# Hyperbolic attention in a four-stage layer: e to the minus x as VectorE's reciprocal of e to the x, in place of ScalarE's second exponential

## The reference

```python
def poincare_fully_connected(x, z, r, c):          # c = 1
    lam = 2.0 / (1.0 - c * sum(x * x))
    z_norm = maximum(norm(z, axis=0), EPS)
    inner = x @ (z / z_norm)
    v = 2.0 * z_norm * arcsinh(lam * inner * cosh(2 r) - (lam - 1.0) * sinh(2 r))
    w = sinh(v)
    return w / (1.0 + sqrt(1.0 + c * sum(w * w)))
Q, K = poincare_fully_connected(x, z_q, b_q, C), poincare_fully_connected(x, z_k, b_k, C)
V = x @ w_v.T + b_v
scores = einsum('bhqd,bhkd->bhqk', Qh, Kh) / sqrt(D_K)        # 16 heads of 16
out = einsum('bhqk,bhkd->bhqd', softmax(scores), Vh)
```

## Time and profile before

| what | value |
|---|---|
| median of 3 runs | 3054.15 us (3049.62 to 3060.38) |
| profiled execution, its own time | 3049.65 us |
| its span, first to last instruction | 3047.8 us |
| ScalarE busy over the span | 2020.5 us (66%) |
| TensorE busy | 2722.6 us (89%) |
| VectorE busy | 1872.9 us (61%) |
| GpSimd busy | 1281.3 us (42%) |
| attention loop, first to last probability | 1446.3 to about 2650 us |

### The profile page before, as it was taken

The page is one execution under the profiler, slowest core; times in us unless marked ns, Lnnn a source line. Parts: engine busy times, 40 slices in busy tenths (PEclk is TensorE's granted clock), DMA queues, the critical chain, the costliest instruction groups (busy, mean ns, idle before and its releaser), DMA issues. The chain is left out here.

```text
span 3047.8 us, 53922 instructions
## 1 busy us (share of the span) xinstructions
PE 2722.6 (89%) x20897; PEld 1231.4 (40%) x20897; DVE 1872.9 (61%) x2420; ACT 2020.5 (66%) x2650; POOL 1281.3 (42%) x786
## 2 busy tenths in 40 slices
PE   2799989999997999953999999999999999789997
PEld 1355555555554444321333333333333332244443
DVE  8899999999994445356455554555555441144444
ACT  6454554555433655531989999999999999745564
POOL 3798998899892122025323232323232220022110
PEclk7899999999998999976999999999999999989999
DMA  2010010001003121123455554545454546232112
GB/s 83 1 35 25 24 41 28 28 28 34 14 21 105 42 69 55 55 82 66 74 96 101 90 106 83 113 78 119 77 119 74 109 70 123 55 96 70 42 41 69
DMA packets 164051, 201.20 MB, mean 66 GB/s; under 512 B 16504, under 2 KB 118272, under 8 KB 163840
## 3 DMA queue, kind: packets, MB, share of 16 engines
q1 hardware_dynamic: 163840, 198.25, 28.8%
HBM read 139.49 MB, written 58.72 MB: 65 GB/s over the span
## 5 line engine op out<-in xcount | busy, mean ns | idle before, releaser
L1870 ACT ACTIVATE b_pr<-b_ps 128x1024 f32<-128x1024 f32 x1024 | 1000.2, 1035 | 141.9 <-PE b_ps L1889 136.1
L1889 PE MATMUL b_ps<-b_st 128*32 128x512 bf16 x8192 | 610.0, 381 | 36.1 <-ACT b_pr L1870 27.8
L1955 PE MATMUL b_acc<-b_pr,b_vaug 128*32 128x512 f32 x4096 | 529.4, 592 | 3.5 <-DVE b_osb L1758 3.2
L1889 PEld LDWEIGHTS b_ps<-b_st 128*32 128x32 bf16 x8192 | 178.9, 95 | 592.0 <-ACT b_pr L1870 357.1
L1257 PE MATMUL f_po<-f_s,f_w 128*128 128x512 f32 x768 | 353.4, 602 | 9.6 <-DVE f_xr L1042 5.9
L1030 DVE TENSOR_TENSOR f_turned<-f_cs,f_s 128x1024 f32<-128x1024 f32 x96 | 119.4, 1243 | 364.0 <-ACT f_cs L1159 359.0
L635 PE MATMUL a_pv<-a_xnT,a_wv 128*128 128x512 f32 x512 | 252.0, 616 | 53.1 <-DVE a_mem L403 38.9
L1123 ACT ACTIVATE f_h<-f_po,f_b 128x512 f32<-128x512 f32 x192 | 131.9, 687 | 216.5 <-PE f_po L1257 216.5
L627 PE MATMUL a_pu<-a_xnT,a_wk 128*128 128x512 f32 x512 | 236.7, 606 | 29.4 <-DVE a_frac L355 23.4
L1586 POOL TENSOR_TENSOR b_SQ<-b_A 128x1024 f32<-128x1024 f32 x32 | 66.7, 2084 | 454.8 <-DVE b_A L1683 454.8
L674 PE MATMUL a_py<-a_wo,a_out 128*128 128x256 f32 x960 | 229.0, 382 | 0.0
(11 more groups left out here) (261 smaller groups left out, 4548.3 us busy)
## 6 DMA issues: line engine op xcount, KB each, us to landing
b_st<-b_scratch SPq DMA_DIRECT2D x512, 128.0 KB, 7.1
b_scratch<-b_parts SPq DMA_DIRECT2D x32, 768.0 KB, 5.2
f_xl<-x SPq DMA_DIRECT2D x16, 1024.0 KB, 5.5
f_xr<-x SPq DMA_DIRECT2D x16, 1024.0 KB, 6.8
a_xl<-in_L_attn_a_x_dram SPq DMA_DIRECT2D x16, 512.0 KB, 4.2
x<-a_xr SPq DMA_DIRECT2D x32, 256.0 KB, 2.2
x<-f_xr SPq DMA_DIRECT2D x8, 1024.0 KB, 4.5
b_xl<-x SPq DMA_DIRECT2D x8, 1024.0 KB, 9.2
```

Source lines behind the costliest of these rows:

```text
L1870: nc.scalar.activation(pr[:, 4 * (blk % 2) + j, :], ps[:, j % 2, :], ACT.Exp, scale=SC).then_inc(S["probs_done"], 1)
L1889: x = nc.tensor.matmul(o[r:r + 32], w[:, r:r + 32], v, start=start, stop=stop, skip_group_check=True)
L1955: x = nc.tensor.matmul(acc[32 * j:32 * j + 32, h * 512:(h + 1) * 512], vaug[:, kt, c:c + 32], pr[:, 4 * (kt % 2) + j, h * 512:(h + 1) * 51 ...
```

## The change

ScalarE no longer takes part in `down`. The step's new first half is an instruction of VectorE: the reciprocal of `EP`, which holds e to the x, written to `SQ`. VectorE waits for `e_done` before it (the exponential of `up`) and signals a new semaphore, `inverted`. GpSimd's subtraction waits for `inverted` in place of `e_done`. `e_done` now counts one per tile, not two. The column of negative scales, `zn2m`, is dropped with the instruction that made it. The place of `down` in the tables stays.

```diff
-ACT_KINDS = ("square", "root", "ln", "up", "down")
+ACT_KINDS = ("square", "root", "ln", "up")
...
                     if kind == "down":
-                        pool.wait_ge(S["e_done"], 8 * b + 2 * i + 2)
+                        pool.wait_ge(S["inverted"], 4 * b + i + 1)
                         nc.gpsimd.tensor_tensor(SQ[:, i, :], EP[:, i % 2, :], SQ[:, i, :], ALU.subtract).then_inc(S["d_done"], 1)
...
+                    if kind == "down":
+
+                        dve.wait_ge(S["e_done"], 4 * b + i + 1)
+                        nc.vector.reciprocal(SQ[:, i, :], EP[:, i % 2, :]).then_inc(S["inverted"], 1)
                     if kind == "sign":
...
                 link(nc.vector.tensor_scalar(zn2, znc, 2.0, None, ALU.mult))
-                link(nc.vector.tensor_scalar(zn2m, znc, -2.0, None, ALU.mult))
...
-                act.wait_ge(S["setup_v"], 11)
+                act.wait_ge(S["setup_v"], 10)
...
                     if kind == "up":
-                        act.wait_ge(S["ln_done"], 4 * b + i + 1)
                         n = 4 * b + i
+                        act.wait_ge(S["ln_done"], n + 1)
...
-                    if kind == "down":
-                        act.wait_ge(S["e_done"], 8 * b + 2 * i + 1)
-                        nc.scalar.activation(SQ[:, i, :], SQ[:, i, :], ACT.Exp, scale=zn2m[:, i:i + 1]).then_inc(S["e_done"], 1)
```

More of the change, by code:

```diff
@@ L1434, in phase_b @@
         rcol, znc, tanh2, ep2, em2, kap, sh, zt = (cols[:, i, :] for i in range(8))
-        zn2, zn2m = cols[:, 3, :], cols[:, 4, :]
+        zn2 = cols[:, 3, :]
         names = ("w_loaded setup_p setup_v setup_a setup_m xl_loaded xr_loaded stored stats_done mv_done rstd_done "
@@ L1439, in phase_b @@
                  "d_done sign_done d2_done pair_done fsum_done froot_done fac_done dfac_done split_done parts_done "
-                 "scores_ready probs_done pv_done acc_taken vaug_done out_mul out_step").split()
+                 "scores_ready probs_done pv_done acc_taken vaug_done out_mul out_step inverted").split()
         S = {n: s.sem(n) for n in names}
```

## The result

The changed kernel takes 3082.86 us (median; 3079.51 to 3088.82), the kernel before on the same chip 3053.16 us: ratio 1.0096, 95% interval 1.0072 to 1.0121. It is 29.7 us slower. The forecast was 3079 us, from terms that sum to 27.3 us of growth. The profiled execution of after took 3088.82 us (span 3087.0), that of before 3049.65 (span 3047.8).

| stretch | before | after | difference | forecast |
|---|---|---|---|---|
| up to the first `square` of stage b | 1353.64 | 1359.03 | +5.4 | 0 |
| from there to the first probability | 92.62 | 118.14 | +25.5 | +25.2 |
| attention loop, first to last probability | 1203.5 | 1214.1 | +10.6 | +2.1 |
| behind it | 398.0 | 395.7 | -2.3 | 0 |

A forecast was written before the change was run, and what follows sets the result against it. It took ScalarE and TensorE as near full in the attention loop, the chain alone deciding in the prologue and block 22. 3049.65 + 25.2 + 2.1 = 3077.0, forecast between two bases at 3079 us, range 3060 to 3110.

The forecast's parts named there:

- The price: Reciprocal of 128x1024 on VectorE: 6.55 us, from a line through three small reciprocals, 152 ns plus 6.25 ns per element.
- Both bounds: Limits on the reciprocal's time: 1.23 us as an ordinary VectorE operation, 16.1 us from the 16-element row spread per element.
- Part 1, the prologue: Four reciprocals lengthen the serial chain on VectorE and GpSimd before the first scores: +25.2 us.
- Part 2, ScalarE's gain: Attention loop, blocks 6, 11, 15 and 18 get shorter without `down` on ScalarE: at most -2.6 us in each of seven batches.
- the rival "gain kept": Block 22 of each batch isn't reached late and ScalarE's gain is kept: 3059 us, chance 0.08.
- Part 3, where the gain goes: Loop: late pairs hold TensorE's sums before block 22, taking back ScalarE's saving: +0.3 us per batch, +2.1 us over seven.
- The upper bound of this part: Loop: the delays of the two sums added up, +1.0 us per batch.
- rival (c): VectorE and GpSimd hold each other up, at an `abs` in block 13: +5.3 us in six batches, 3111 us, chance 0.12.
- The sum: Whole kernel: 3049.65 + 25.2 + 2.1 = 3077.0 us for the profiled execution; forecast put at 3079 us.
- Sensitivity: Each microsecond more on a reciprocal costs four in the prologue and two per batch in seven batches: 18 us.
- Rival (b): Each reciprocal takes 2 us longer than the line: +36 us, 3115 us, chance 0.08.
- Rival (a): The reciprocal streams like other VectorE operations, 1.23 us; prologue +4.3, 2.3 us per batch kept: 3038 us, chance 0.08.

The follow-up runs named there:

- the one that has this part alone: Changed kernel with only the prologue's four inversions as reciprocals, the loop's 28 back on ScalarE's exponential: 3076.65 us, 1.0085 against the kernel before.
- The short operation: Changed kernel with an ordinary VectorE operation of the same shape in place of the reciprocal, e to the minus x not formed: 3048.45 us, 0.9985.
- the kernel with the later subtraction: Kernel without exponential or reciprocal for `down`, plus one wait: GpSimd's subtraction of tile 1 waits for VectorE's `y` addition for tile 2: 3044.88 us, 0.9971.
- The kernel with tile 3 alone: Against the kernel with reciprocals in the loop only: just tile 3's inversion of each loop batch stays a reciprocal: 3059.22 us, 1.0019 to the kernel before.
- its stand-in, 2.15 us longer: Changed kernel with a second reciprocal of 320 elements ahead of each full one: 3143.67 us, 1.0297 against the kernel before.

## Why the prediction was right, and where it wasn't

**The price (6.55 us): right.** 6540 ns against 6552. The line through 4, 8 and 16 elements held to 1024, and at 320 too (152 + 6.25 x 320 = 2152 ns against 2140 in the mean). Both bounds were far off, the value between them was known to 0.2%. The prediction's estimate from the repeat count of 8 that the Trainium skill gives ("VectorE: DVE Perf Modes", First, the fixed hardware budget) was 8.53 us. The trace doesn't agree: 6540 ns for 1024 elements are 6.1 cycles of the 0.96 GHz given there per element, 6.0 without the fixed part.

**Part 1, the prologue (+25.2): right**, +25.5 in the changed kernel and +25.7 in the one that has this part alone. It holds because the chain there is serial and every piece had a row.

**Part 2, ScalarE's gain (at most 2.6 per batch): too large.** The short operation and the kernel with the later subtraction both show 1.68. The step that failed is the count by block, in which every block with a `down` comes down to the 4.17 us of block 19 and blocks 6 and 15 are like block 11. Block 6 gave 0.66 and block 11 0.33 instead of 0.5 each, block 15 nothing instead of 0.5, as TensorE sets its pace anyway, and block 18 0.67 instead of 1.10. It did no harm to the forecast, as the gain is taken back anyway, but the rival "gain kept" would have come out at 3079 - 2.1 - 7 x 1.68 = 3065 us and not 3059.

**Part 3, where the gain goes (+0.3 per batch): right in place and size**, +0.4: 1.66 us are saved in blocks 6, 11 and 18, and 2.05 lost in block 20. The forecast times of the steady batch, all in the scale of the earlier trace rows, against after: first reciprocal end 2124.1 against 2123.88, `pair0` end 2141.7 against 2140.67, that of block 18 2147.1 to 2153.65 against 2147.28 to 2153.82, `sign3` end 2157.7 against 2157.70, `pair1` end 2162.1 against 2162.16. One step was wrong in it: `pair0` came a microsecond earlier than worked out, TensorE waited 0.16 us there and not 1.3, so the first sum takes back little; the second does it all (1.90 us). The kernel with tile 3 alone shows the same: its chain in block 18 is enough for the whole cost. The upper bound of this part, +1.0, isn't the sum of the two delays that it names: 2141.7 - 2141.57 and 0.33 make 0.5.

**What the forecast lacked: single long batches.** The 7.8 us of the profiled execution are rival (c) in kind, VectorE and GpSimd holding each other up, but not in place. It was put on `abs` in block 13, with every batch paying. `abs` got better instead, from a mean of 1417 ns before to, in the groups by line of after,

```profile
L1692 DVE TENSOR_SCALAR b_EP<-b_A 128x1024 int32<-128x1024 int32 x32 | 33.3, 1042 | 0.5
```

with its longest in the loop down from 2876 to 2155 ns. The victim was the addition of the output (L1778), an operation of no weight in any table of before: median 426 ns, longest 2120 then, 4081 now. By these overlaps, what decides whether a batch pays is where it starts against GpSimd's row of operations, which no run varied by itself; in the batch of 159.67 a gap of 1.10 us in TensorE, to which the profile gives no releaser, stood ahead of it. Whether the four executions of after, from 3079.5 to 3088.8, differ by the number of such batches is likely but was not seen, as only one was profiled.

**The sum.** 3077.0 worked out for the profiled execution, 3088.8 measured: 5.4 from the stages ahead of the change, +0.3 prologue, +8.5 loop, -2.3 behind it. The median lies nearer, 3.9 us over the forecast. On the median of before, 3054.15, the same terms give 3081.5. The growth of the medians is 29.7 against 27.3, so the nearness is mostly the mechanism's; the long batches, which no term held, lie in what is left. The measured ratio of 1.0096 answers to the 0.8% given.

**Sensitivity (18 us per us of reciprocal): wrong.** Measured 61/2.15 = 28 us. It was right for the prologue (4) and wrong for the loop, where "two per batch" holds only while the covers of blocks 6 and 11 hold (some 1.7 us of slack were named for one of them); beyond that it is 3.9. Rival (b) was priced by it at 3115; its stand-in, 2.15 us longer, took 3143.67.

**Rival (a)** was forecast at 3038; its stand-in gave 3048.45, 0.15% faster than before (by 5.4 us). The stand-in reads its input twice and was held up by GpSimd, the reciprocal reads it once. At the 4.3 us that the prediction gives the prologue it would have been some 2 us faster still, an estimate from the 6.5 measured, and still far from 3038: of the gain of 2.3 per batch only 1.68 is there.

## What to carry to other kernels

Fit a line through the small sizes of an operation in the trace and go by it: here it was right to 0.2% over a factor of 64, while a bound from the nearest ordinary operation was off by five. Before moving work from a near-full engine to a half-idle one, look for the stretches where the half-idle one is itself the chain: 32 operations moved, and the four in the prologue made 25.5 of the 29.7 us lost. In a hand-ordered pipeline a cost in the loop can be a threshold and not a slope: here find the one step whose chain sets the end (tile 3), leave it where it is, and the rest of the move may even pay. Measure block by block what a saving is worth: four equal operations taken from ScalarE gave 0.66, 0.33, 0 and 0.67 us.

## What the runs showed of the hardware

- VectorE's reciprocal in float32 takes 152 ns and 6.25 ns per element: 177, 202, 252, 2140 and 6540 ns at 4, 8, 16, 320 and 1024 elements in each of 128 partitions. In the loop all 28 took 6516 to 6555 ns, the twelve beside which GpSimd worked for 1.5 to 4.2 us as well as the sixteen beside which it stood idle, and the `pair0` that lies wholly inside the reciprocal from 2022.89 to 2029.43 took 2.37 us, where it was 2.57 before. That agrees with the Trainium skill ("SBUF — State Buffer", Who interferes with whom), by which an operation with one SBUF input outside the two-port modes doesn't contend.
- A VectorE addition with two SBUF inputs can be held through several GpSimd operations in a row: 0.42 us became 4.08 (two operations) and 5.43 (three). One of 1.23 us became 3.20 beside a single GpSimd subtraction, and was 1.23 again when a wait kept that away. The same section of the Trainium skill calls the ports that the two engines share an exclusive lock, over which an instruction with two SBUF inputs contends with a GpSimd instruction that reads SBUF. The runs agree, and show a hold of more than one such instruction.
- Leaving work out can cost time: without any `down` GpSimd's subtraction moved into VectorE's additions, and the kernel took 3060.9 us; with one wait more, 3044.88.
